# Matmuls of the slot counts behind the second pair's scores, and VectorE's offsets and slots one iteration later, in a fused patch embedding, attention and expert kernel

## The chip, the core and the metric

The kernel runs on one core of a Trainium2 chip: TensorE (matmuls into PSUM banks), VectorE, ScalarE and GpSimd, the queues that issue DMA (SyncE's above all), and 16 DMA engines. Each engine works through its own instructions in the order in which they are written; semaphores tie the engines together. The metric is the device time of the core in microseconds (us), lower is better.

## What is computed

32 images of 224x224 are cut into 16x16 patches, embedded into 192 numbers each, put along a Hilbert curve of 256 places and joined with 77 text tokens: 333 tokens an image. Then comes a block of convolutional attention and a block of experts, each behind a layer norm and added to its input. Cut to what matters:

```python
h = concat([patch_embed(x)[:, hilbert], txt], 1)            # (32, 333, 192)
q = layernorm(h)
key  = pointwise(depthwise9(q)) + pw_b                      # 12 heads of 16
w    = softmax(einsum(key * q, ak_w) + ak_b)                # 9 taps per head
v    = q @ pt_w.T + pt_b
h    = h + sum_k w[..., k] * shift(v, k)
f    = layernorm(h)
scores, idx = top_k(f @ Wg, 2); weights = softmax(scores)   # 8 experts
for k in range(2):                                          # capacity 1598 each
    pos = cumsum(onehot(idx[:, k])) - 1                     # place within the expert
    buf[e, pos] = token (dropped beyond capacity)
    ye  = (f[buf] @ W1a * silu(f[buf] @ W1b)) @ W2
    out = out.at[buf].add(w_buf * ye)
```

The running count over all tokens (`cumsum`) gives each token its slot in an expert's list. It goes on from group to group: the order of the groups is fixed by it.

## The kernel before

There are two stages. The first makes rows and slots (to about 830 us), the second runs tiles of 256 slots through the experts. The change lies in the first.

The first stage works in 16 **pairs** of images (p) and 8 **groups** of four images (g). Iteration `it` of its loop runs pairs p = 2it and p + 1 through embedding, transposes, convolutions, values and scores; beside it VectorE runs the window sums of group it - 1, and the routing of group h = it - 2 is under way. Every engine has this loop written out in an order of its own.

TensorE, per iteration: for each of three tiles t, `conv(p, t)` (nine taps of 333 columns into `bankK`) and `values(p, t)` (into `bankV`); `transposes(p + 1)`; `patch(p + 2)` (48 matmuls into `bankH`); the three chunks of `scores(p, c)` into `bankN`; then the same for p + 1, with the transposes and the logits of group h between the taps of two convolutions; `transposes(p + 2)`, `patch(p + 3)`; `counts_before(h)` (L1090, L1091), two small matmuls that sum the counts over partitions into columns 448 to 479 of `bankN`; and `scores(p + 1, c)` (L1049). Logits, scores and counts share `bankN`. So `scores` waits before its first chunk until VectorE has read the logits (`lg_read`) and the counts (`pre_read`), and each chunk waits until ScalarE has emptied the one ahead (`kern_evac`).

VectorE, per iteration: `attend(p, 0)` (L666 reads `bankK`, L671 reads `bankV`), `norm(p + 1)` (L644, L652, L658), `part(2)`, `attend(p, 1)`, `softmax_top(it - 1)` (L693, L695, L697), `attend(p, 2)`, `part(14)`, `softmax_end` (L703 to L707), `attend(p + 1, 0)`, `norm(p + 2)`, `part(6)`, `attend(p + 1, 1)`, `part(8)`, `attend(p + 1, 2)`, `top_two(h)` (L761 to L790: the two best experts, their difference `gap` at L784, the counts `cnt` at L789), `part(2)`, `offsets(h)` (L796, L797: reads the counts out of `bankN` and adds `pre_read`), `places(h)` (L805 to L847: slots and weights of each token, `idx_ready`), `part(7)`. `part(n)` takes n steps of the window sums: a product (L713), a sum (L731), or the statistics of a finished slice (L748, L755). 39 steps an iteration are all that a group has, plus one; they are in two slices.

ScalarE, per iteration: `normalise(p + 1)`, the exponential of the window softmax (L563), the copies out of the transposes' banks (`tiles_out`, L519), `scores_out(p)` (L528, L530), the normalising of a slice (L540), copies for the router (L559), `normalise(p + 2)`, `tiles_out(p + 2)`, the gate's exponential of `gap` (L567), `scores_out(p + 1)`, `high_parts` (L549), and the next slice.

GpSimd, per iteration: layer norms of a pair or a slice (four small steps, L405 to L411), `low_parts` (L428, L429) and the 22 scatters (L129) of group it - 3, which wait for `idx_ready`, in two portions of 7 and 15. SyncE stores each pair's rows once its scores are emptied and loads the windows of a group behind both stores.

## Time and profile before

| | us |
|---|---|
| runs (three) | 1452.49, 1452.85, 1455.80 |
| median | 1452.85 |
| the profiled execution | 1455.03 |
| its span in the profile | 1453.2 |
| first stage, until the expert stage's first matmul | 836.5 |
| distance of the counts (L1090) of two iterations | 79.8, 81.4, 81.0, 79.9, 76.0 |

The profiled execution is one of its own. Its durations are read in the rows below, and the 1.8 us between its time and its span lie outside the records. A row of the timeline has its start, its length, the engine, the line and operation, what is written and read, how often it comes in a row, and in brackets how long the engine had been idle and what ended that. Mean granted TensorE clock of the whole execution: 0.907 of full speed.

### The profile page before, as it was taken

What the parts mean: (1) busy time and instruction counts of PE and PEld (TensorE: products, weight loads), DVE (VectorE), ACT (ScalarE), POOL (GpSimd) and SP (SyncE); (2) the same over time, 40 slices, a digit from 0 to 9 for tenths busy, and PEclk for the clock granted to TensorE, in tenths of its full rate; (3) what the DMA queues carried; (4) which work ended last, traced back from release to release, by engine and by line L of the source; (5) the groups of instructions that cost most, each with busy time, mean ns of one, the idle gap of its engine ahead of it and who ended that gap; (6) DMA issues with size and microseconds to landing.
All of it is one profiled execution on the core that took longest, in us unless ns stands there. A gap on an engine that the chain in (4) does not pass through costs nothing. (4 is left out here: it accounts for less than half of the span.)

```text
span 1453.2 us, 30800 instructions
## 1 busy us (share of the span) xinstructions
PE 1206.9 (83%) x8700; PEld 1012.7 (70%) x8701; DVE 1017.8 (70%) x2367; ACT 463.6 (32%) x1197; POOL 694.9 (48%) x530
## 2 busy tenths in 40 slices
PE   6987988998989898960642099999999999999995
PEld 6766777775767677640422078988898898898895
DVE  4117958999999999999576266666666666666663
ACT  2111222323223232311112254444444444444442
POOL 1000221666656666755647625544545454555454
PEclk9999999898999899885675599999999999999998
DMA  9995554565646363548611175544444444444442
GB/s 314 401 320 135 141 151 113 161 177 166 169 119 196 101 187 84 162 98 220 190 46 49 48 131 67 65 58 59 64 63 55 65 57 63 57 63 58 62 60 28
DMA packets 215171, 175.31 MB, mean 121 GB/s; under 512 B 121864, under 2 KB 198694, under 8 KB 215104
## 3 DMA queue, kind: packets, MB, share of 16 engines
q1 hardware_dynamic: 170128, 115.36, 32.7%
q0 software_dynamic: 34720, 34.38, 14.3%
q10 hardware_dynamic: 10256, 24.73, 4.6%
q8 instruction: 36, 0.59, 0.2%
q14 instruction: 31, 0.25, 0.1%
HBM read 69.24 MB, written 88.47 MB: 109 GB/s over the span
## 5 line engine op out<-in xcount | busy, mean ns | idle before, releaser
L1239 POOL DMA_INDIRECT out<-yb,meta x182 | 301.5, 1657 | 314.0 <-DMA out<-yb,meta 207.2
L129 POOL DMA_INDIRECT expert_inputs<-slot_rows,slots x176 | 236.5, 1344 | 85.5 <-issue 60.1
L1023 PE MATMUL bankK<-normedT,conv_w 128*128 128x333 f32 x864 | 277.2, 469 | 0.0
L1312 DVE TENSOR_TENSOR hidden<-silu,bankU 128x256 f32<-128x256 f32 x364 | 153.0, 421 | 136.6 <-PE bankU L1352 90.3
L1268 ACT ACTIVATE silu<-bankG 128x256 f32<-128x256 f32 x364 | 139.1, 383 | 301.7 <-PE bankG L1352 301.6
L1023 PEld LDWEIGHTS bankK<-normedT,conv_w 128*128 128x128 f32 x864 | 168.8, 201 | 77.7 <-issue 12.1
L1365 PE MATMUL bankY<-expert_weights,hidden_high 128*128 x728 | 179.2, 246 | 0.9 <-issue 0.2
L1366 PE MATMUL bankY<-expert_weights,hidden_high 128*128 x728 | 179.3, 246 | 0.0
L1367 PE MATMUL bankY<-expert_weights,hidden_low 128*128 x728 | 179.1, 246 | 0.0
L713 DVE TENSOR_TENSOR prod<-window_values,kb 128x960 f32<-128x960 f32 (+1 forms) x135 | 167.8, 1252 | 3.6
L731 DVE TENSOR_TENSOR hidden_group<-hidden_group,prod 128x960 f32<-128x960 f32 (+1 forms) x135 | 169.0, 1252 | 0.5
L1306 DVE TENSOR_TENSOR hidden_low<-hidden,hidden_high 128x256 f16<-128x256 f32 x364 | 153.1, 421 | 12.6
L1264 ACT CAST hidden_high<-hidden 128x256 f16<-128x256 f32 x364 | 145.2, 399 | 49.2 <-DVE hidden L1312 49.1
L1348 PE MATMUL bankG<-xeT,expert_weights 128*128 128x256 f16 x364 | 99.9, 275 | 68.5 <-DMA xeT<-expert_inputs 58.0
L1001 PE MATMUL bankH<-wp_sb,patches 128*128 128x192 f32 x768 | 138.7, 345 | 10.3 <-DMA tokb_sb<-in_tokb 10.3
L405 POOL TENSOR_TENSOR tmp<-mean_var,pool_constants 128x6 f32<-128x6 f32 (+1 forms) x32 | 24.3, 760 | 255.6 <-DVE mean_var L658 233.5
L1001 PEld LDWEIGHTS bankH<-wp_sb,patches 128*128 128x128 f32 x768 | 135.5, 204 | 9.9 <-DMA tokb_sb<-in_tokb 9.9
L1288 DVE TENSOR_SCALAR yb<-bankY,slot_weight 128x192 f32<-128x192 f32 x182 | 67.5, 412 | 62.4 <-PE bankY L1367 62.4
L1348 PE MATMUL bankU<-xeT,expert_weights 128*128 128x256 f16 x364 | 100.0, 275 | 0.0
L1352 PE MATMUL bankG<-xeT,expert_weights 128*128 128x256 f16 x364 | 99.7, 274 | 0.0
L1350 PE MATMUL bankG<-xeT,expert_weights 128*128 128x256 f16 x364 | 99.7, 274 | 0.0
L1349 PE MATMUL bankG<-xeT,expert_weights 128*128 128x256 f16 x364 | 99.7, 274 | 0.0
(162 smaller groups left out, 2294.9 us busy)
## 6 DMA issues: line engine op xcount, KB each, us to landing
patches<-in_x SPq DMA_DIRECT2D x16, 1536.0 KB, 8.9
expert_inputs<-prod ACTq DMA_DIRECT2D x6, 3430.0 KB, 23.3
token_rows<-rowbuf SPq DMA_DIRECT2D x32, 492.0 KB
window_values<-token_rows SPq DMA_DIRECT2D x32, 264.0 KB, 5.5
hidden_group<-token_rows SPq DMA_DIRECT2D x32, 264.0 KB, 7.1
window_values<-token_rows SPq DMA_DIRECT2D x32, 192.0 KB, 5.7
kb<-token_rows SPq DMA_DIRECT2D x32, 148.5 KB, 4.7
token_rows<-rowbuf SPq DMA_DIRECT2D x32, 148.0 KB
```

What stands on the lines that cost most here:

```text
L129: nc.gpsimd.indirect_dma_start(out=xslots[:, :], out_offset=bass.IndirectOffsetOnAxis(ap=idx[g % 2][:, k, r:r + 1], axis=0), in_=xrow[g % ...
L713: return V.tensor_tensor(to[:, 0:(hi - lo) * D].rearrange("p (a d) -> p a d", d=IPG), vx[g % 2][:, (lo + k) * D:(hi + k) * D].rearrange("p ...
L731: added[k] = done(V.tensor_tensor(acc, acc, prod[k % 2][:, 0:(hi - lo) * D], ALU.add))
L1001: mm = T_.matmul(bankH[c][:, m * D:(m + 1) * D], xb[u][:, m, kc * TI + c * 128:kc * TI + c * 128 + 128], wp_sb[:, kc, :], start=(kc == 0), ...
L1023: mm = T_.matmul(bankK[(u + t) % 2][:, 0:L], conv_w[:, t // 2, k, :], qT[u][:, t, k:k + L], start=(k == 0), stop=(k == K - 1))
L1239: nc.gpsimd.indirect_dma_start(out=out[:, :], out_offset=bass.IndirectOffsetOnAxis(ap=meta[t % NMETA][:, c, 0:1], axis=0), in_=yb[v][:, c, ...
L1306: V.tensor_tensor(hl[v][:, j, :], hf[j % 2][:, :], hh[v][:, j, :], ALU.subtract)\
L1312: V.tensor_tensor(hf[j % 2][:, :], sg[j % 2][:, :], bankU[j][:, 0:TS], ALU.mult)\
L1348: T_.matmul(o, w(0, lo), high, start=True, stop=False)
L1365: T_.matmul(o, hh[v][:, j, cs], w(0, j), start=(j == 0), stop=False)
L1366: T_.matmul(o, hh[v][:, j, cs], w(1, j), start=False, stop=False)
L1367: mm = T_.matmul(o, hl[v][:, j, cs], w(0, j), start=False, stop=(j == NJ - 1))
```

## The change

On TensorE the counts of group h move behind the three chunks of `scores(p + 1)`. They then wait until ScalarE has emptied the last chunk (`2 * g + 6` pairs of `kern_evac` in place of `2 * g + 5`). `scores` no longer waits for the counts of its own iteration to be read, but for those of the iteration before, now in both pairs. On VectorE, `offsets` and `places` of a group are made in the following iteration, behind `norm(p + 1)`; `part(2)` and `part(7)` become `part(9)`. Those of group 5 come behind the loop, ahead of the rest of group 6's window sums.

```diff
--- before.py
+++ after.py
@@ -927,6 +927,9 @@
                     attend(p, 0)
                     if it:
                         norm(p + 1)
+                    if it > 2:
+                        offsets(h - 1)
+                        places(h - 1)
                     if it > 1:
                         part(2)
                     attend(p, 1)
@@ -949,13 +952,11 @@
                     attend(p + 1, 2)
                     if it > 1:
                         top_two(h)
-                    part(2)
-                    if it > 1:
-                        offsets(h)
-                        places(h)
-                    part(7 if it > 1 else 13)
+                    part(9 if it > 1 else 15)
 
                 g, h = NG - 1, NG - 2
+                offsets(h - 1)
+                places(h - 1)
                 part(2 * NSL * K)
                 softmax_top(g)
                 softmax_end(g)
@@ -1041,9 +1042,10 @@
                     u = p % 2
                     pe.wait_ge(ca_done, 3 * p + 3)
                     wait(pe, kern_evac, 3 * p + c)
-                    if c == 0 and p > 3 and p % 2:
-                        pe.wait_ge(lg_read, p // 2 - 1)
-                        pe.wait_ge(pre_read, p // 2 - 1)
+                    if c == 0 and p > 3:
+                        if p % 2:
+                            pe.wait_ge(lg_read, p // 2 - 1)
+                        wait(pe, pre_read, p // 2 - 2)
                     T, n = CT[c], HA * K
                     for t in range(3):
                         mm = T_.matmul(bankN[0:T, t * n:(t + 1) * n], ca[u][:, t, 128 * c:128 * c + T],
@@ -1086,7 +1088,7 @@
 
                 def counts_before(g):
                     pe.wait_ge(cnt_ready, g + 1)
-                    pe.wait_ge(kern_evac, 3 * min(2 * g + 5, NPAIR))
+                    pe.wait_ge(kern_evac, 3 * min(2 * g + 6, NPAIR))
                     T_.matmul(bankN[:, CN:CN + 16], low_sb[:, :], cnt[:, :], start=True, stop=True)
                     T_.matmul(bankN[:, CN + 16:CN + 32], ones[:, 0:128], cnt[:, :], start=True, stop=True)\
                       .then_inc(pre_ready, 1)
@@ -1120,10 +1122,10 @@
                         transposes(p + 2)
                     if p + 3 < NPAIR:
                         patch(p + 3)
+                    for c in range(3):
+                        scores(p + 1, c)
                     if it > 1:
                         counts_before(h)
-                    for c in range(3):
-                        scores(p + 1, c)
 
                 g, h = NG - 1, NG - 2
                 for _ in logits(h, NPAIR):
```

TensorE at the end of an iteration's second pair, from the counts to the next pair's first convolution (`bankN` holds scores, logits and counts). Before:

```order
L1090 MATMUL bankN<-cnt,lower_sb 128x16 [waits kern_evac,cnt_ready]
L1091 MATMUL bankN<-cnt,ones 128x16
L1049 MATMUL bankN<-akA_sb,conv_attn_64 128x72 [waits lg_read,pre_read,kern_evac,ca_done]
L1049 MATMUL bankN<-akA_sb,conv_attn_64 128x72
L1049 MATMUL bankN<-akB_sb,conv_attn_64 128x72
L1049 MATMUL bankN<-akA_sb,conv_attn_64 128x72 [waits kern_evac,ca_done]
L1049 MATMUL bankN<-akA_sb,conv_attn_64 128x72
L1049 MATMUL bankN<-akB_sb,conv_attn_64 128x72
L1049 MATMUL bankN<-akA_sb,conv_attn_64 77x72 [waits kern_evac,ca_done]
L1049 MATMUL bankN<-akA_sb,conv_attn_64 77x72
L1049 MATMUL bankN<-akB_sb,conv_attn_64 77x72
L1023 MATMUL bankK<-normedT_61,conv_w 128x333 [waits ca_done,qT_done]
```

And with the change:

```order
L1051 MATMUL bankN<-akA_sb,conv_attn_64 128x72 [waits lg_read,pre_read,kern_evac,ca_done]
L1051 MATMUL bankN<-akA_sb,conv_attn_64 128x72
L1051 MATMUL bankN<-akB_sb,conv_attn_64 128x72
L1051 MATMUL bankN<-akA_sb,conv_attn_64 128x72 [waits kern_evac,ca_done]
L1051 MATMUL bankN<-akA_sb,conv_attn_64 128x72
L1051 MATMUL bankN<-akB_sb,conv_attn_64 128x72
L1051 MATMUL bankN<-akA_sb,conv_attn_64 77x72 [waits kern_evac,ca_done]
L1051 MATMUL bankN<-akA_sb,conv_attn_64 77x72
L1051 MATMUL bankN<-akB_sb,conv_attn_64 77x72
L1092 MATMUL bankN<-cnt,lower_sb 128x16 [waits kern_evac,cnt_ready]
L1093 MATMUL bankN<-cnt,ones 128x16
L1024 MATMUL bankK<-normedT_61,conv_w 128x333 [waits ca_done,qT_done]
```

The two counts matmuls stand behind the nine of the scores now, and the first score matmul keeps its four waits, `pre_read` with a smaller number.

VectorE from the end of `top_two` to the second attend of the next iteration (`off` and `base` are the first steps of `offsets`, `token_numbers` the last of `places`, `stats<-rowbuf` belongs to `norm`). Before:

```order
L790 SCALAR_TENSOR_TENSOR running_count<-ones,onehot_valid 128x176
L731 TENSOR_TENSOR hidden_group<-hidden_group,prod 128x1152 [waits vector_step]
L713 TENSOR_TENSOR prod<-window_values,kb 128x1152 [waits vector_step]
L796 TENSOR_TENSOR off<-bankN,base 128x16 [waits pre_ready]
...
L847 TENSOR_SCALAR token_numbers<-token_numbers 128x11
...
L748 BN_STATS stats<-hidden_group 128x6 [waits vector_step]
...
L666 SCALAR_TENSOR_TENSOR conv_attn_63<-bankK,pwb_sb,normedT_61 128x333 [waits kern_ready,key_ready]
...
L644 TENSOR_TENSOR rowbuf_58<-bankH,tokb_sb 128x2x192 [waits h_ready,row_stored1]
...
L658 BN_AGGR mean_var<-stats 128x2 x5
...
L666 SCALAR_TENSOR_TENSOR conv_attn_63<-bankK,pwb_sb,normedT_61 128x333 [waits kern_ready,key_ready]
```

And with the change:

```order
L790 SCALAR_TENSOR_TENSOR running_count<-ones,onehot_valid 128x176
L731 TENSOR_TENSOR hidden_group<-hidden_group,prod 128x1152 [waits vector_step]
L713 TENSOR_TENSOR prod<-window_values,kb 128x1152 [waits vector_step]
...
L748 BN_STATS stats<-hidden_group 128x6 [waits vector_step]
...
L666 SCALAR_TENSOR_TENSOR conv_attn_63<-bankK,pwb_sb,normedT_61 128x333 [waits kern_ready,key_ready]
...
L644 TENSOR_TENSOR rowbuf_58<-bankH,tokb_sb 128x2x192 [waits h_ready,row_stored1]
...
L658 BN_AGGR mean_var<-stats 128x2 x5
L796 TENSOR_TENSOR off<-bankN,base 128x16 [waits pre_ready]
...
L847 TENSOR_SCALAR token_numbers<-token_numbers 128x11
...
L666 SCALAR_TENSOR_TENSOR conv_attn_63<-bankK,pwb_sb,normedT_61 128x333 [waits kern_ready,key_ready]
```

The 22 steps from `off` to `token_numbers` have gone from ahead of the slice's statistics to behind the norm, past the first attend; the second attend has the same steps ahead of it as before. ScalarE, GpSimd and SyncE keep their orders.

## Rows read from the trace of the kernel before

**Rows 1.** The page: busy time, share of the span and instructions of each engine.
```profile
PE 1206.9 (83%) x8700; PEld 1012.7 (70%) x8701; DVE 1017.8 (70%) x2367; ACT 463.6 (32%) x1197; POOL 694.9 (48%) x530
```

**Rows 2.** Windows: us, busy time of five engines, TensorE clock, DMA share, GB/s.
```profile
250.00:330.00 80.00, 72.39 (x356) 57.55 (x356) 76.22 (x144) 23.09 (x57) 49.65 (x41) 0.91 0.57 157
...
492.00:572.00 80.00, 72.57 (x353) 57.30 (x354) 76.29 (x143) 23.09 (x57) 51.39 (x43) 0.91 0.51 140
```

**Rows 3.** Waits of VectorE, 250 to 650 us: total us, times, longest.
```profile
DVE kb L693 <- DMA window_values<-token_rows: 1.9, 3, 0.9
DVE rowbuf L671 <- PE bankV L1037: 1.7, 4, 0.7
DVE stats L652 <- DMA rowbuf<-in_txt: 1.6, 1, 1.6
...
DVE conv_attn L666 <- PE bankK L1023: 1.2, 1, 1.2
```

**Rows 4.** Waits of TensorE, 250 to 650 us.
```profile
PE bankN L1049 <- DVEq L799: 13.8, 5, 2.8
```

**Rows 5.** Timeline of TensorE (start, us, work), two stretches of scores.
```profile
531.71 0.56 PE L1049 MATMUL bankN<-akA_sb,conv_attn 128*128 128x72 f32 x4
...
535.00 6.89 PE L1023 MATMUL bankK<-normedT,conv_w 128*128 128x333 f32 x18
...
563.02 8.01 PE L1001 MATMUL bankH<-wp_sb,patches 128*128 128x192 f32 x48
571.88 0.40 PE L1090 MATMUL bankN<-cnt,lower_sb 128*128 128x16 f32 x2 [0.85 <-DVE cnt L789]
...
575.26 0.64 PE L1049 MATMUL bankN<-akA_sb,conv_attn 128*128 128x72 f32 x4 [2.76 <-DVEq L799]
...
579.77 6.70 PE L1023 MATMUL bankK<-normedT,conv_w 128*128 128x333 f32 x18
```

**Rows 6.** Timeline of VectorE around offsets and places.
```profile
570.94 0.16 DVE L784 TENSOR_TENSOR gap<-m 128x11 f32<-128x11 f32 x1
...
574.82 0.16 DVE L796 TENSOR_TENSOR off<-bankN,base 128x16 f32<-128x16 f32 x1
...
578.94 1.35 DVE L731 TENSOR_TENSOR hidden_group<-hidden_group,prod 128x1152 f32<-128x1152 f32 x1
```

**Rows 7.** Timeline of ScalarE, the window softmax's exponential.
```profile
521.94 1.20 ACT L563 ACTIVATE kb<-kb 128x1188 f32<-128x1188 f32 x1 [0.15 <-DVE kb L697]
```

**Rows 8.** Timeline of TensorE, the last transpose of the first half.
```profile
361.11 0.82 PE L1013 MATMUL bankT<-identity,normed 128*128 128x128 f32 x3 [2.13 <-ACT normedT L519]
361.72 9.24 PE L1001 MATMUL bankH<-wp_sb,patches 128*128 128x192 f32 x48
...
523.52 0.51 PE L1013 MATMUL bankT<-identity,normed 128*128 128x128 f32 x3 [0.88 <-ACT normedT L519]
```

**Rows 9.** Windows: the clock behind that wait.
```profile
361.00:364.00 3.00, 2.89 (x10) 2.89 (x11) 2.93 (x4) 0.83 (x3) 2.69 (x2) 0.50 0.18 63
```

**Rows 10.** Timeline of VectorE at four places.
```profile
381.09 0.57 DVE L666 SCALAR_TENSOR_TENSOR conv_attn<-bankK,pwb_sb,normedT 128x333 f32<-128x333 f32 x1 [1.24 <-PE bankK L1023]
...
519.59 2.32 DVE L697 TENSOR_TENSOR kb<-kb,kmax 128x1188 f32<-128x1188 f32 x1
...
671.78 2.59 DVE L731 TENSOR_TENSOR hidden_group<-hidden_group,prod 128x960 f32<-128x960 f32 x1
...
684.02 0.44 DVE L755 BATCH_NORM_AGGREGATE mean_var<-stats 128x2 f32<-128x6 f32 x5
```

**Rows 11.** Timeline of GpSimd at four places.
```profile
519.02 1.64 POOL L429 TENSOR_TENSOR slot_rows<-group_normed,slot_rows 128x768 f16<-128x768 f32 x1
...
660.17 1.02 POOL L405 TENSOR_TENSOR tmp<-mean_var,pool_constants 128x6 f32<-128x6 f32 x1 [0.17 <-DVE mean_var L755]
...
670.80 2.55 POOL L429 TENSOR_TENSOR slot_rows<-group_normed,slot_rows 128x768 f16<-128x768 f32 x1
...
693.30 0.22 POOL L405 TENSOR_TENSOR tmp<-mean_var,pool_constants 128x5 f32<-128x5 f32 x1
```

## The prediction

> **What bounds the kernel now.** I first read the busy line of the page [rows 1]: TensorE 83%, VectorE 70% of the whole span. That average hides two stages. The change touches only the first 830 us, so the windows of single iterations of the first loop come next [rows 2]: from 250 us on, VectorE is busy 76 of every 80 us and TensorE 72. What VectorE does with the other 4 us is in its list of waits [rows 3]. From 250 to 650 us, five iterations, it waits 6.4 us for anybody: 1.9 for window loads, 1.7 for `bankV`, 1.6 for the text load, 1.2 for `bankK`. The rest, some 2 to 3 us an iteration, are the small gaps between dependent steps of its own. So **VectorE sets the length of iterations 3 to 7**, and TensorE's stalls are time that it has to spare. TensorE does wait, 13.8 us in five places, for exactly what the change takes away [rows 4]. But an engine that waits because another is full gains only what the full one gives back.
>
> **The stall that is removed.** In the iteration that ends at 579.77, TensorE finishes the patch matmuls at 571.03, gets the counts in at 571.88, idles 2.76 us until VectorE has read them (two window steps stand ahead of that read), and starts the scores at 575.26 and the next convolution at 579.77: 8.74 us [rows 5]. With the scores first, the first chunk can start at 571.1. The second needs ScalarE to empty `bankN`, and ScalarE has the gate's exponential ahead of that copy in its own order. That exponential waits for `gap`, which VectorE has at 571.10 [rows 6]. From there 0.2 us of exponential, 0.45 of copies, two more chunks as in the first pair's scores (531.71 to 535.00 for all three, 3.29 us [rows 5]), then a new wait: the counts need the last chunk emptied (some 0.6 us), and take 0.6 themselves. The convolution starts at 576.0 to 577.0, **2.8 to 3.8 us earlier**. Queued behind the counts' new wait are only that convolution and what follows it.
>
> **The steps that are moved on VectorE.** Offsets and places take from 574.82 to 578.94, 4.12 us [rows 6]. They are neither shorter nor fewer, and the two window steps that stood ahead of them stay. The second half of the group's first slice, its statistics, the first attend and the norm of the next iteration all come 4.12 us earlier; from the second attend on VectorE stands where it stood. Is the first attend's data there 4.12 us earlier? It began right when `bankV` was ready before; now the convolution starts at 576.0 to 577.0, takes 6.7 us at the mixed clock [rows 5] and 1.3 for the values, so 584.0 to 585.0, and VectorE wants `bankV` at about 584.8. It just fits: 0, bounds 0 to +1.5 for five iterations. The counts themselves were written 8 us or more before offsets now reads them: no wait. GpSimd's scatter needs the slots that places makes. It stands behind a layer norm and two subtractions there, and places ends about when that norm does: nothing.
>
> **Where the lead goes.** Behind the third convolution TensorE transposes the next pair. The last of the three transposes needs a bank that ScalarE empties, and ahead of that copy ScalarE has the window softmax's exponential, which waits for VectorE's subtraction, ending at 521.9. That time has not moved. So the exponential still starts at 521.94 [rows 7] and the last transpose, which waited 0.88 us at 523.52 [rows 8], still starts there: the wait grows to 4 to 5 us and **the lead is gone**. Window loads are the exception: they hang on the stores behind the second pair's scores, so they arrive 3 to 5 us earlier, and VectorE's waits for them go: **-1.9 us** [rows 3] (bounds 0 and -1.9). Its other waits hang on work behind that transpose and stay.
>
> **A price of the longer idle.** After 2.13 us without work at 361.11 [rows 8] the granted clock is 0.50, that is 1.2 instead of 2.4 GHz, until 364 [rows 9]. The patch matmuls took 9.24 us there and 8.01 in the other iteration [rows 5, 8]. VectorE then waited 1.24 us for `bankK` [rows 10] and 0.67 for `bankV`, where others have 0.36 in all: 1.55 us more. A wait of 4 to 5 us will do the same in iterations 3, 5 and 6 (4 has it already; 7 has no patch matmuls and 5 us of slack): 3 x 1.55 = **+4.65 us**. Bounds: 0 if the clock holds, and twice the row's price in those three and once more in 4, 7 x 1.55 = +10.9.
> The Trainium skill ("TensorE: Matmul & The Clock Gate", HAM oscillation) says the same: an idle gap between bursts re-throttles the array, and the next burst starts cold each time. By that rule this term is certain and the slower case below gains; by the shorter waits of the trace alone it could be left at 0.
>
> **GpSimd against VectorE.** VectorE's subtraction of 1188 elements took 2.32 us at 519.59 against 1.40 at other places, while GpSimd's L429 ran to 520.66 [rows 10, 11]: 0.92 lost, and 4.7 us over the five iterations, 0.94 each. At 671.78 a window step of 1.15 us took 2.59 beside L429 [rows 10, 11], and the one before it lost 0.6: 2.04 in all. These subtractions of GpSimd follow its layer norm, which starts with the norm of VectorE and so now 4.12 us earlier. They meet the steps of places, many of them with two inputs, instead of a reduction and one subtraction. Between 0.94 and 2.04 I take the middle, 1.49: 5 x 0.55 = **+2.75 us**, bounds -4.7 (they miss each other) and 5 x 1.10 = +5.5.
> The Trainium skill ("SBUF — State Buffer", Who interferes with whom) gives the reason: a VectorE instruction with two SBUF inputs and a GpSimd instruction that reads SBUF take turns on one port, and whoever comes second waits for the whole instruction. The rows agree, and by the rule a chain of small two-input steps can lose to both subtractions, which is the upper bound.
>
> **The end of the first stage.** Here the move does help. In the last iteration places of group 5 stood ahead of the statistics of group 6's first slice, and now stands behind them. GpSimd's norm of that slice starts at 660.17 and would start at 656.1. Behind it follow on GpSimd the low parts and seven scatters, and only then the norm of the second slice, at 693.30, although VectorE had its input at 684.46 [rows 10, 11]. On this norm hang ScalarE's exponential of the last group, VectorE's last windows, and the scatters that hold back the expert stage. Ten us of slack on VectorE's side, so all of it moves: **-4.1 us**. SyncE's weight loads also start some 5 us earlier (the last scores are emptied at 651.7 instead of 656.9), and the 8.6 us hole in the scatters goes with them; bounds -4.1 and -5.2.
>
> **The sum.** -1.9 + 4.65 + 2.75 - 4.1 = +1.4 us. The profiled execution took 1455.03 us (span 1453.2), 2.2 above the median of 1452.85; a difference carries over, so 1452.85 + 1.4 = **1454.2 us**. A measurement here can tell about 0.3%, 4.4 us, from no change.
>
> **Rivals.**
> 1. Neither clock nor port costs anything. Then -1.9 - 4.1 = -6.0 gives 1446.9, and with all of VectorE's waits gone and the end at its bound -6.4 - 5.2, 1441.3. For it: the clock held through the waits of 1.4 us. Against: it fell after 2.1, and 4 to 5 are longer. 0.16.
> 2. TensorE is the bound after all, and the 2.8 to 3.8 us count in each of four iterations: 4 x 3.3 + 4.1 = 17.3, so 1435.5. Against it stand 6.4 us of VectorE waits in 400. 0.04.
> 3. Slower. The transposes' idle time costs a long slow stretch each time: +10.9 + 2.75 - 1.9 - 4.1 = +7.65, 1460.5; with the port at its bound 1463.3. It decides once the losses of the loop pass 4.4 + 6.0 = 10.4 us, which is 2.1 us an iteration. For it: the clock has only two levels, and a longer idle time can put the whole patch group and the scores behind it at the lower one. 0.20.
> 4. The change does not do what it says: ScalarE's order holds the scores back as long as the counts did, nothing moves in the loop, and only the end gains: 1448.7. 0.05.
> The forecast has 0.55. Faster by over 0.3%: rivals 1 and 2, 0.20. Slower: rival 3, 0.20. Within: 0.60. The range that leaves out one in ten at either side runs from inside rival 1, 1445.5, to inside rival 3, 1461.5.
>
> **What would show it.** In the profile after: no wait of TensorE's scores for VectorE's queue; a wait of 4 to 5 us of the last transpose for `normedT`, with the granted clock at 0.5 behind it; patch matmuls of the first half at 9 us or more; VectorE's waits for `bankK` at four iterations instead of one, and none for window loads; its busy time an iteration up by 0.5; counts 80 to 83 us apart; the norm of the last but one group's second slice 4 us earlier beside VectorE's last window step. I am wrong if iterations become shorter than 79 us (TensorE's lead reached VectorE), or if that norm stays where it was.

## The result and the profile after

The kernel before takes 1452.49 us (median of 7 runs, 1450.62 to 1455.8) and the changed kernel **1460.14 us** (7 runs, 1454.15 to 1462.41): ratio 1.0043, 95% interval 1.0028 to 1.0057, so 6.2 us more by the ratio (the medians are 7.7 apart). The forecast was 1454.2, 1.4 us more. A second pair gave 1.0025 (1.0011 to 1.0039), and a third, on another chip than the second, 1.0127 (1.0106 to 1.0147). The change is slower each time, and in the third by far the most; both want an explanation.

Each group of four experiments below ran on one chip, beside the kernel before. The median of the kernel before was 1461.60 us in the first group, 1454.48 in the second and 1454.31 in the third. The profiled execution of the changed kernel took 1454.15 us, its fastest; that of before took 1455.03, one of its slower ones. So the two traces differ by 0.9 us only, and I compare stretches of them, not their ends. A further trace of each comes from one chip (`before_again`, 1454.21, and `again2`, 1459.37).

The busy line of the changed kernel's page answers to [rows 1]:

```profile
PE 1202.0 (83%) x8700; PEld 1009.5 (70%) x8701; DVE 1024.8 (71%) x2367; ACT 463.3 (32%) x1197; POOL 671.4 (46%) x530
```

GpSimd has 23 us less, VectorE 7 us more. VectorE's step `gap` (L784) marks the same work in each iteration, and the five iterations that the prediction spoke of lie between the `gap` of iteration 2 and that of iteration 7, the last. Windows from mark to mark (us, busy time of each engine, TensorE's granted clock, DMA share, GB/s), first before and `before_again`, then after and `again2`:

```profile
248.91:646.89 397.98, 348.73 (x1655) 272.91 (x1655) 377.41 (x697) 110.56 (x273) 252.80 (x206) 0.91 0.54 148
```

```profile
246.28:645.85 399.57, 349.90 (x1655) 273.25 (x1655) 378.62 (x698) 110.62 (x273) 252.37 (x206) 0.90 0.54 147
```

```profile
246.47:651.35 404.88, 346.17 (x1655) 271.72 (x1655) 383.71 (x698) 110.05 (x273) 228.20 (x206) 0.92 0.53 145
```

```profile
247.41:654.69 407.28, 347.40 (x1660) 272.98 (x1659) 383.68 (x698) 110.11 (x273) 227.70 (x206) 0.92 0.53 145
```

The loop is **6.9 us longer** in the first pair (`before`, `after`) and 7.7 in the second (`before_again`, `again2`), and VectorE's busy time alone has grown by 6.3 and 5.1 us. Where it grew is in the groups by line of the same stretches, before and then after:

```profile
L731 DVE TENSOR_TENSOR hidden_group<-hidden_group,prod 128x1152 f32<-128x1152 f32 x45 | 60.7, 1348 | 0.2
...
L697 DVE TENSOR_TENSOR kb<-kb,kmax 128x1188 f32<-128x1188 f32 x5 | 11.1, 2217 | 0.2
...
L825 DVE TENSOR_TENSOR pos<-onehot_valid,merged 128x176 f32<-128x176 f32 x5 | 1.7, 342 | 0.2
...
L831 DVE TENSOR_SCALAR keep<-posk 128x22 f32<-128x22 f32 x5 | 0.8, 167 | 0.0
```

```profile
L731 DVE TENSOR_TENSOR hidden_group<-hidden_group,prod 128x1152 f32<-128x1152 f32 x45 | 63.1, 1401 | 0.2
...
L697 DVE TENSOR_TENSOR kb<-kb,kmax 128x1188 f32<-128x1188 f32 x5 | 7.0, 1395 | 0.2
...
L831 DVE TENSOR_SCALAR keep<-posk 128x22 f32<-128x22 f32 x5 | 5.6, 1125 | 0.0
L825 DVE TENSOR_TENSOR pos<-onehot_valid,merged 128x176 f32<-128x176 f32 x5 | 5.5, 1093 | 0.2
```

The softmax's subtraction (L697) lost its delay, 4.1 us in all, and the softmax's first step (L693) another 0.6, which that step had in one iteration. Two steps of places took the delay over and more: L825 went from 0.34 to 1.09 us and L831 from 0.17 to 1.13, 8.6 us in all. And two window adds (L731) beside GpSimd's subtractions for the second slice take 3.2 us instead of 2.7, five times, 2.4 in all. Together that is the 6.3 us. GpSimd in one of these places, and VectorE beside it:

```profile
512.97 0.91 POOL L428 TENSOR_TENSOR slot_rows<-group_normed,slot_rows 128x384 f16<-128x384 f32 x1
513.84 1.74 POOL L429 TENSOR_TENSOR slot_rows<-group_normed,slot_rows 128x768 f16<-128x768 f32 x1
```

```profile
512.99 1.09 DVE L825 TENSOR_TENSOR pos<-onehot_valid,merged 128x176 f32<-128x176 f32 x1
...
514.49 1.13 DVE L831 TENSOR_SCALAR keep<-posk 128x22 f32<-128x22 f32 x1
```

From the first step of offsets to the last of places it is now 5.74 us instead of 4.05, in each of the five iterations. VectorE's waits, as in [rows 3]:

```profile
DVE stats L652 <- DMA rowbuf<-in_txt: 5.1, 4, 1.4
...
DVE rowbuf L671 <- PE bankV L1038: 1.4, 4, 0.4
```

The waits for window loads are gone, and so is the one for `bankK`; one of 0.5 us for a store of rows is new. But the **text load** now holds it up four times, 5.1 us instead of 1.6. TensorE, as in [rows 4]:

```profile
PE bankT L1014 <- ACT normedT L519: 18.7, 9, 3.5
...
PE bankV L1036 <- DVE rowbuf L671: 12.5, 5, 2.7
```

The 13.8 us behind `offsets` are gone; what the lead ran into stands here. The last transpose of each first half waits 3.55 us for ScalarE, `values(p, 2)` 2.4 to 2.7 us for VectorE's second attend. What follows that transpose, to be held against [rows 5, 8]:

```profile
525.47 0.51 PE L1014 MATMUL bankT<-identity,normed 128*128 128x128 f32 x3 [3.55 <-ACT normedT L519]
525.82 9.69 PE L1002 MATMUL bankH<-wp_sb,patches 128*128 128x192 f32 x48
...
538.59 5.25 PE L1024 MATMUL bankK<-normedT,conv_w 128*128 128x333 f32 x18
```

```profile
520.00:534.00 14.00, 12.10 (x76) 10.91 (x74) 13.83 (x13) 4.52 (x12) 12.11 (x7) 1.00 0.36 140
534.00:546.00 12.00, 11.49 (x46) 8.08 (x46) 11.10 (x25) 3.53 (x10) 3.73 (x5) 0.86 0.70 213
```

```profile
520.00:534.00 14.00, 10.45 (x55) 9.84 (x55) 13.79 (x14) 2.30 (x4) 7.68 (x5) 0.88 0.12 42
534.00:546.00 12.00, 10.84 (x56) 8.39 (x55) 11.18 (x20) 3.49 (x11) 1.78 (x4) 1.00 0.44 148
```

The first two windows are of the kernel before, the last two of the changed one. The patch matmuls take 9.69 us where [rows 5] has 8.01, with a granted clock of 0.88 over these 14 us instead of 1.00. But the convolution behind the scores, which took 6.89 us at 0.86, now has 1.00 and takes 5.25. **In this iteration, number 6, the clock falls once either way, only earlier.**

In the trace of before, iterations 3 and 6 have the fall behind the scores. Iteration 5 has it at the patch matmuls already, behind a wait of 0.88 us, and iteration 4 has two falls. The patch matmuls of iteration 4 and the convolution behind its scores, then the patch matmuls of iteration 5:

```profile
361.00:371.00 10.00, 9.89 (x54) 9.89 (x54) 9.83 (x10) 0.83 (x3) 8.78 (x5) 0.84 0.14 48
374.00:381.00 7.00, 7.00 (x24) 4.60 (x22) 5.49 (x13) 2.69 (x7) 1.78 (x4) 0.76 0.75 250
442.00:452.00 10.00, 9.94 (x53) 9.94 (x53) 9.83 (x10) 0.78 (x3) 8.78 (x5) 0.83 0.13 47
```

In the first trace of the changed kernel iterations 3 to 6 all have 0.83 at the patch matmuls and 1.00 behind the scores. The mean over the whole loop, in the windows from mark to mark above, is 0.92 in both traces of the changed kernel, 0.91 and 0.90 in those of before: in these two pairs the change costs no clock.

The end of the stage, to be held against [rows 10, 11]:

```profile
651.35 0.16 DVE L784 TENSOR_TENSOR gap<-m 128x11 f32<-128x11 f32 x1
```

```profile
692.33 0.86 POOL L405 TENSOR_TENSOR tmp<-mean_var,pool_constants 128x5 f32<-128x5 f32 x1
```

```profile
836.73 0.39 PE L1350 MATMUL bankG<-xeT,expert_weights 128*128 128x256 f16 x1 [57.98 <-DMA xeT<-expert_inputs]
```

From the last `gap` of the loop to GpSimd's norm of the last slice there are 41.0 us instead of 46.4. To the first matmul of the expert stage there are 185.4 instead of 189.6 (836.45 less 646.89 before), and 186.1 instead of 190.8 in the second pair.

### The profile page after: what moved, and what is told of

Same layout as the page of the kernel before. It is cut to its first block and busy times, and to the rows that moved or that the text cites. A ratio compares the mean times of both kernels' runs of the same rounds, so it can differ in the third digit from the quotient of the medians.

```text
span 1452.4 us, 30799 instructions
## 1 busy us (share of the span) xinstructions
PE 1202.0 (83%) x8700; PEld 1009.5 (70%) x8701; DVE 1024.8 (71%) x2367; ACT 463.3 (32%) x1197; POOL 671.4 (46%) x530
## 5 line engine op out<-in xcount | busy, mean ns | idle before, releaser
L129 POOL DMA_INDIRECT expert_inputs<-slot_rows,slots x176 | 220.1, 1251 | 91.8 <-issue 60.2
L731 DVE TENSOR_TENSOR hidden_group<-hidden_group,prod 128x960 f32<-128x960 f32 (+1 forms) x135 | 171.5, 1271 | 0.5
L405 POOL TENSOR_TENSOR tmp<-mean_var,pool_constants 128x6 f32<-128x6 f32 (+1 forms) x32 | 20.9, 652 | 307.6 <-DVE mean_var L658 234.3
L1002 PEld LDWEIGHTS bankH<-wp_sb,patches 128*128 128x128 f32 x768 | 136.5, 205 | 10.2 <-DMA tokb_sb<-in_tokb 10.2
```

The lines of the kernel that those rows point to most:

```text
L129: nc.gpsimd.indirect_dma_start(out=xslots[:, :], out_offset=bass.IndirectOffsetOnAxis(ap=idx[g % 2][:, k, r:r + 1], axis=0), in_=xrow[g % ...
L731: added[k] = done(V.tensor_tensor(acc, acc, prod[k % 2][:, 0:(hi - lo) * D], ALU.add))
L1002: mm = T_.matmul(bankH[c][:, m * D:(m + 1) * D], xb[u][:, m, kc * TI + c * 128:kc * TI + c * 128 + 128], wp_sb[:, kc, :], start=(kc == 0), ...
```

## Experiments

**again.** The changed kernel, unaltered, in the first group.

> The changed kernel once more, unaltered, for a second trace: its first trace was of a run of 1454.15 us, while its median was 1460.14. Theory A (clock): typical runs are slower because the granted clock falls behind the longer wait of the last transpose at 0.5 and stays there over the patch matmuls, so that VectorE waits for bankK in three iterations or more, 1 to 1.5 us each; then this trace, if its run took 1458 us or more, shows L671 or L666 waiting for bankK for 3 us or more between 250 and 650 us. Theory B (text load and port): no bankK wait again, VectorE's waits for the text load 5 us in all, places 5.7 us instead of 4.05 in every iteration, and the extra of a typical run lies outside the first loop. Ratio to the kernel before under both 1.003 to 1.006.

1481.42 us, ratio 1.0127 (1.0106 to 1.0147), three times the excess of the first result and outside what both theories expected. VectorE's waits in the loop:

```profile
DVE stats L652 <- DMA rowbuf<-in_txt: 7.5, 4, 2.6
DVE conv_attn L666 <- PE bankK L1024: 6.6, 4, 2.3
DVE rowbuf L671 <- PE bankV L1038: 4.1, 8, 0.7
```

The waits for `bankK` that theory A asked for are there, but their cause is not the one it named. ScalarE and TensorE at the end of an iteration (`gap` at 505.12), and GpSimd's last scatter of the row:

```profile
505.32 0.21 ACT L567 ACTIVATE ex<-gap 128x11 f32<-128x11 f32 x1 [9.14 <-DVE gap L784]
509.71 0.28 ACT L528 COPY rowbuf<-bankN 128x144 f32<-128x144 f32 x1 [4.18 <-remote]
```

```profile
503.38 0.56 PE L1051 MATMUL bankN<-akA_sb,conv_attn 128*128 128x72 f32 x4
...
510.26 1.10 PE L1051 MATMUL bankN<-akA_sb,conv_attn 128*128 128x72 f32 x4 [6.09 <-ACT rowbuf L530]
...
514.81 1.46 PE L1024 MATMUL bankK<-normedT,conv_w 128*128 128x333 f32 x2
```

```profile
507.10 1.44 POOL L129 DMA_INDIRECT expert_inputs<-slot_rows,slots  x1 [0.30 <-issue]
```

The first chunk of scores is computed by 504.2 and ScalarE is free from 505.5, yet its copy starts at 509.71: 4.18 us in which nothing that the profile shows is missing. The convolution starts 9.7 us after `gap` instead of 4.3 in the first trace (578.45 after 574.14), and VectorE stands at the first attend. I call this the stall. It happens in iterations 3 to 6. In iterations 2 and 7, where no scatters are in progress, the copy follows the exponential at once, and in the first trace it does so always. The copy starts 1.1 to 1.3 us after the end of the last scatter, in all four.

The loop of this trace takes 421.85 us, 17.0 more than in the first. About 11 of these are VectorE's waits, and 5.9 are busy time (389.62 us instead of 383.71): GpSimd's subtractions for the second slice come later too and meet window steps of 960 elements, which take 110.5 us in all instead of 103.3.

**tail_only.** The kernel before with the last iteration of the change.

```diff
-                    if it > 1:
+                    if 1 < it < NG - 1:
                         offsets(h)
                         places(h)
...
                 g, h = NG - 1, NG - 2
+                offsets(h - 1)
+                places(h - 1)
                 part(2 * NSL * K)
...
-                    if it > 1:
+                    if 1 < it < NG - 1:
                         counts_before(h)
                     for c in range(3):
                         scores(p + 1, c)
+                    if it == NG - 1:
+                        counts_before(h)
```

> The kernel before with the change in its last iteration only: the counts of group 5 behind the last scores, and offsets and places of group 5 behind the loop; all earlier iterations are the kernel before. Theory A (the term of the end is real and separate): the distance from the last gap of the loop to GpSimd's norm of group 6's second slice falls from 46.4 us to 41 or 42, all but 1 us of it reaches the first expert matmul, and the time is 1447.5 to 1448.5 us, ratio 0.9965 to 0.9975. Theory B (something else is late next at the end: ScalarE's scores or the window sums of the last group): ratio 0.999 to 1.001. Theory C (the shorter end in the first trace was not the move but what the loop left behind, for instance its earlier stores): the distance stays at 45 to 46.

1455.39 us, ratio **0.9954** (0.9937 to 0.9970). The distance from `gap` (649.38) to the norm (691.97) is 42.6 us. Theory A holds for the distance and the sign; the gain was 6.2 us where it had said 4 to 5. The trace does not show where those arrive: from `gap` to the first expert matmul it has 192.6 us, more than `before` and `before_again` (189.6 and 190.8), but `again` has 192.9 on this chip, of whose kernel before there is no trace. VectorE waits 0.56 to 0.74 us for the counts in iterations 3 to 6 of this trace, as it does in neither of the two traces of before. There too it goes on 1.1 to 1.3 us after the last scatter.

**slots_first.** GpSimd's scatters ahead of its low parts.

```diff
-                    if it > 1:
-                        low_parts(it - 2, 0)
                     if it > 2:
                         scatter(it - 3, 0)
+                    if it > 1:
+                        low_parts(it - 2, 0)
```

> The changed kernel with one edit: in the loop GpSimd issues the first scatters of a group ahead of the low parts of the next group's first slice, and so begins these two subtractions only when VectorE has made the slots. Theory A (VectorE and GpSimd share a port, and places loses to these subtractions): the two steps that took 1.09 and 1.13 us take 0.34 and 0.17 again and places 4.1 us instead of 5.7 in all five iterations, 1.6 us each; if the subtractions then meet nothing as dear, 8 us less than the changed kernel; if the moved subtractions take from VectorE's maximum and subtractions of the softmax what they took before, 0.9 each, 3.5 us less (ratio 1.002 instead of 1.0043). Theory B (the longer steps come from something else, for instance their own place behind the norm): places stays at 5.7 and the time at ratio 1.004.

1473.62 us, 7.8 less than `again` on the same chip. Groups of `again` and then of this one:

```profile
L731 DVE TENSOR_TENSOR hidden_group<-hidden_group,prod 128x960 f32<-128x960 f32 x45 | 56.6, 1257 | 0.2
L713 DVE TENSOR_TENSOR prod<-window_values,kb 128x960 f32<-128x960 f32 x45 | 53.9, 1207 | 1.2
...
L831 DVE TENSOR_SCALAR keep<-posk 128x22 f32<-128x22 f32 x5 | 5.6, 1124 | 0.0
L825 DVE TENSOR_TENSOR pos<-onehot_valid,merged 128x176 f32<-128x176 f32 x5 | 5.5, 1092 | 0.2
```

```profile
L713 DVE TENSOR_TENSOR prod<-window_values,kb 128x960 f32<-128x960 f32 x45 | 60.5, 1354 | 1.2
L731 DVE TENSOR_TENSOR hidden_group<-hidden_group,prod 128x960 f32<-128x960 f32 x45 | 60.1, 1336 | 0.2
...
L825 DVE TENSOR_TENSOR pos<-onehot_valid,merged 128x176 f32<-128x176 f32 x5 | 1.7, 342 | 0.2
...
L831 DVE TENSOR_SCALAR keep<-posk 128x22 f32<-128x22 f32 x5 | 0.8, 163 | 0.0
```

Places is back at 4.03 us, 8.6 less in all. **GpSimd's subtractions are what places loses to.** Moved, they meet the window steps of the second slice and cost 10.1 us there, beyond the 7.2 that these steps lose in `again` already. VectorE's busy time is no smaller (390.93 us against 389.62), and still the kernel is faster, because places stands ahead of the softmax's subtraction. ScalarE waits 5.58 us for that instead of 7.29, the last transpose, the scores and the stores come earlier, and the waits for the text load fall from 7.5 to 2.1 us.

**patch_first.** TensorE's patch matmuls ahead of the transposes.

```diff
-                    transposes(p + 1)
                     if p + 2 < NPAIR:
                         patch(p + 2)
+                    transposes(p + 1)
```

> The changed kernel with one edit: TensorE does the patch matmuls of pair p+2 ahead of the transposes of pair p+1 instead of behind them, so the wait of the last transpose for ScalarE is filled with work. Theory A (that idle time costs through the clock and through the later scores, stores and text load): the 3.55 us wait goes below 0.5, the patch matmuls take 8 us or less instead of 9.7, the first pair's scores are ready 3 us earlier, VectorE's waits for the text load fall from 5.1 us to about 1.5 between 250 and 650 us, and the time is 3.5 us less than the changed kernel, or 7 where typical runs have bankK waits besides. Theory B (the transposes are now late for ScalarE's copies, which hold the second pair's convolution): VectorE waits for bankK or bankV 1 us or more in every iteration, 0 to 5 us more than the changed kernel.

1465.26 us, 16.2 less than `again` (ratio 1.0031, 1.0018 to 1.0045). The last transpose waits 0.24 us instead of 3.55, the scores of the first half start 41.6 us after `gap` instead of 46.7 (534.05 less 492.42, 551.78 less 505.12), and VectorE does not wait for the text load at all (7.5 before). What it still waits for is `bankK`, 8.2 us, and `bankV`, 2.9. I put that down to the stall at the end of the iteration, which shows on ScalarE in three iterations here. In the fourth TensorE itself starts its scores late, at 580.71, 1.10 us after the end of the last scatter, idle for 0.78 us before with nothing missing that the profile shows. So theory A holds for the chain from the transposes' wait to the text load, and the gain is twice the 7 us it allowed; what the other half is, no run separates.

**before_again, again2, three_parts, tail_three** (second group). The first two are unaltered. In the other two, four scatters move, in `three_parts` in the changed kernel and in `tail_three` in the kernel of `tail_only`. The same portions are issued behind the loop (not shown):

```diff
-            SC_AT = (0, 7, TOPK * R)
+            SC_AT = (0, 7, 11, TOPK * R)
...
                     if it > 1:
                         slice_norm(it - 2, 1)
+                    if it > 2:
+                        scatter(it - 3, 1)
                     if not last(2 * it + 1):
                         pair_norm(2 * it + 2)
                     if it > 2:
-                        scatter(it - 3, 1)
+                        scatter(it - 3, 2)
```

> The kernel before, unaltered, for a trace beside those of its neighbours. Theory A (a signal of TensorE given while GpSimd issues its row of scatters arrives only about 1.2 us after the last one, and the kernel before is hardly touched since its scores come later anyway): offsets is reached 3.7 us after the gate's exponential, or 4.3 to 4.5 where the signal of the counts is late, and ScalarE's first copy of the second pair's scores comes 5 to 6.5 us after that exponential as in its first trace; time 1451 to 1462 us. Theory B (one chip is simply slower in everything): VectorE's waits between 250 and 650 us grow by several us here too.

> The changed kernel, unaltered, a third trace. In the second one ScalarE stood still for 4.1 to 4.3 us in iterations 3 to 6 between the gate's exponential and the first copy of scores that had been computed 1 to 2 us before the exponential, and went on 1.1 to 1.3 us after the last of GpSimd's scatters each time; in the first trace it did not. Theory A (that stall is what the change exposes, and it makes the difference between the runs): traces with the four stalls take 15 us or more longer than the kernel before, and show VectorE waiting for bankK for 1.3 us or more in each of those iterations; those without it 0 to 3 us more than the kernel before. Theory B (the difference lies in the clock behind the transposes' wait): the time is large with or without the stalls.

1454.21 and 1459.22 us (ratio 1.0025). Neither shows the stall: from the start of the gate's exponential to offsets there are 3.68 us in `before_again`, and in `again2` 0.12 us to the start of the copy in iterations 3 to 6. Yet `again2` is 4.7 us above before by the medians, 3.6 by the ratio, where theory A had 0 to 3. The stall goes with the larger excess of the first group but is not all of it: without it 3 to 6 us are left.

> The changed kernel with one edit: four of GpSimd's fifteen later scatters of a group are issued behind the norm of the slice, where GpSimd has 7.8 us without work, so that the last of the row ends 5.2 us earlier, about 2 us before the gate's exponential instead of 1.4 to 3.4 us behind it. Theory A (the row of scatters holds TensorE's signal back): the copy follows the exponential at once (0.12 us) in every iteration, the scores, stores and text loads come 4 us earlier, and where the unaltered changed kernel shows the stalls the time is 9 to 13 us less than its; where it shows none, 0 to 2 us less. Theory B (ScalarE stalls there for a reason of its own, or because of what it executes): the stall of 4.2 us stays, and the time is that of the changed kernel within 2 us.

1460.24 us, ratio 1.0045 (1.0029 to 1.0061), against 1.0025 (1.0011 to 1.0039) for `again2`: no gain. On this chip there was no stall to take away, so nothing is said on theory A. It was not run on the chip that shows the stall, and **whether the scatters cause the stall stays open**.

> The kernel before with the change in its last iteration only, as in tail_only, and with four of the fifteen later scatters issued behind the slice's norm. Theory A: VectorE no longer waits for the counts (0.56 to 0.74 us in four iterations of tail_only), TensorE waits less for the read of the counts, the row of scatters ends earlier at the end of the stage too; 2 to 5 us less than tail_only, ratio to the kernel before 0.992 to 0.995. Theory B (the four scatters push the pair's norm late, since GpSimd had only 6.6 us free there, and with it normalise and the transposes): the time is that of tail_only or up to 3 us more.

1450.08 us, ratio **0.9972** (0.9962 to 0.9982), 4.1 us less than before by the ratio, and not the 0.992 to 0.995 expected; VectorE waits for no counts. `tail_only` ran on another chip, so whether the moved scatters add anything to the shorter end is not shown. From the last `gap` (645.06) to the first expert matmul (831.23) there are 186.2 us, 4.6 less than in `before_again` on the same chip: here the end's gain is seen to arrive.

**short_after, short_before** (third group): GpSimd's subtractions for the first slice of groups 0 to 5 shrunk to one column; the low parts of these rows stay zero.

```diff
-                    V.memset(xrow[n][:, :, META:XW], 0)
+                    V.memset(xrow[n][:, :, :], 0)
...
                     pool.wait_ge(xh_ready, NSL * g + s + 1)
+                    if s == 0 and g < NG - 2:
+                        nc.gpsimd.tensor_tensor(x16[:, ss, LOB:LOB + 1], xn[:, ss, 128:129], x16[:, ss, 128:129],
+                                                ALU.subtract).then_inc(xl_ready, 1)
+                        return
```

> The changed kernel, in which GpSimd's subtractions for the first slice of groups 0 to 5 write one column instead of 192 each row (the low parts of these rows stay zero, so what the experts receive is not the reference's). It takes away what places meets on GpSimd and nothing else. Theory A (the port): places takes 4.05 us instead of 5.74 in all five iterations, 8.5 us in all, and softmax_top comes as much earlier, with it the exponential, the last transpose, the scores and the text load: 8.5 to 11 us less than the changed kernel, ratio to the kernel before 0.996 to 0.998. Theory B (places is longer for another reason, or the time saved goes into waits): places stays at 5.74, or the ratio is 1.001 or more.

> The kernel before with the same shortened subtractions on GpSimd. Theory A: its VectorE meets them only in the softmax's last subtraction, 2.17 to 2.60 us instead of 1.40, so it gains 0.9 to 1.2 us an iteration, 4.5 to 6 us, ratio 0.996 to 0.997; the change is then worth 3 to 5 us on the port, the difference between the two savings, and the two shortened kernels come within 2 us of one another (the end saves 5, the text load costs 3.5). Theory B (the port is no part of the difference): both shortened kernels save the same, and their distance stays 4 to 6 us.

1448.95 us, ratio 0.9973 (0.9957 to 0.9990), and 1452.59 us, 0.9990 (0.9975 to 1.0005). The loop of short_before, then of short_after:

```profile
247.62:645.31 397.69, 344.23 (x1656) 269.64 (x1655) 373.17 (x697) 109.95 (x273) 230.85 (x201) 0.91 0.54 148
```

```profile
246.87:647.69 400.82, 349.47 (x1662) 274.80 (x1660) 375.48 (x697) 110.23 (x273) 214.31 (x201) 0.92 0.53 147
```

In `short_after` places is back at 4.05 to 4.08 us. With these subtractions gone from both, the change comes out **faster** than the kernel without it, by 3.6 us at the medians and 2.5 by the ratios, whose intervals overlap; with them it was 3.6 to 6.2 slower in the two pairs without the stall. Its loop is still 3.1 us longer (400.82 less 397.69). What makes it faster is the end: 185.9 us from the last `gap` to the first expert matmul, 190.8 in `short_before`.

On the busy time the subtractions cost 5.5 us in the kernel before (378.62 less 373.17; 4.2 by the trace `before`) and 8.2 in the changed one (383.68 less 375.48). What is left between the two short kernels, 2.3, is L731's. But the time they give back is 1.5 us in before, less than the 4.5 to 6 of theory A, and 7.6 or 10.2 after (0.9973 against 1.0025 and 1.0043). These are ratios of other groups, since the changed kernel itself did not run in this one, and with intervals of 2 us at either side the two sizes are rough. In before VectorE's gain went into waits: 5.1 us for the text load and 3.0 for `bankV`, where `before_again` has 2.5 and 2.1. So the text load is not a price of the change alone; it stands right behind VectorE in both kernels.

**pe_only** (third group). TensorE's half of the change; VectorE as before.

```diff
-                    if c == 0 and p > 3 and p % 2:
-                        pe.wait_ge(lg_read, p // 2 - 1)
-                        pe.wait_ge(pre_read, p // 2 - 1)
+                    if c == 0 and p > 3:
+                        if p % 2:
+                            pe.wait_ge(lg_read, p // 2 - 1)
+                        wait(pe, pre_read, p // 2 - 2)
...
-                    pe.wait_ge(kern_evac, 3 * min(2 * g + 5, NPAIR))
+                    pe.wait_ge(kern_evac, 3 * min(2 * g + 6, NPAIR))
...
+                    for c in range(3):
+                        scores(p + 1, c)
                     if it > 1:
                         counts_before(h)
-                    for c in range(3):
-                        scores(p + 1, c)
```

> TensorE's half of the change alone: the counts behind the scores, but VectorE makes offsets and places where the kernel before does. VectorE then waits for counts that come 4.5 us after the gate's difference instead of 1.4, at a place that it reaches after 3.9: 0.6 us or a little more in each iteration, or 4 to 5 where ScalarE's first copy of the scores is held back by GpSimd's scatters. Nothing of the port and nothing of the end's gain. Theory A (VectorE's half causes the loss in the loop and the gain at the end): the waits for window loads vanish (1 to 2 us), 3 us for the counts come, ratio 1.000 to 1.002. Theory B (TensorE's half costs by itself, because the earlier convolution leads to the longer wait of the last transpose and so to later scores and text loads): 1.003 or more.

1469.31 us, ratio **1.0112** (1.0086 to 1.0138). Waits of VectorE, and two steps of places:

```profile
DVE off L796 <- PE bankN L1092: 3.1, 5, 1.0
```

```profile
L812 DVE TENSOR_TENSOR pos<-running_count,off 128x176 f32<-128x176 f32 x5 | 5.0, 994 | 0.2
...
L808 DVE TENSOR_SCALAR w<-ex 128x11 f32<-128x11 f32 x5 | 4.0, 800 | 0.0
```

The counts come 0.4 to 1.0 us late, as both theories had it (3.1 us). The rest was in neither. The earlier scores make ScalarE's high parts and so GpSimd's subtractions for the second slice come earlier, and in this order these meet places. L812 takes 0.99 us instead of 0.34 and L808, eleven elements, 0.80 instead of 0.11: 6.7 us. These two make up the 9.8 us by which the loop (409.36) is longer than in `before_again`; the end has 1.5 more (192.3 instead of 190.8 us to the first expert matmul). Theory B's bound is met, but not by its cause. TensorE's half alone costs 15 to 16 us. The whole change cost 3.6 and 6.2 in the pairs without the stall, and this trace has no stall either, so VectorE's half seems to repair more than it costs. The changed kernel was not run in this group and cost 18.5 us where it met the stall, so that is not shown.

**mended** (third group). The changed kernel with the edits of patch_first, slots_first and three_parts.

> The changed kernel with three edits together: the patch matmuls ahead of the transposes, the slots' scatters ahead of the low parts, and four of the later scatters behind the slice's norm. Theory A (the move gains nothing in the loop even where all its side costs are removed, because VectorE is the bound there): VectorE waits less than 1 us an iteration, the iterations are 78 to 80 us as in the kernel before, and only the end's 5 us are left: ratio 0.996 to 0.998, no better than the version that changes the last iteration alone. Theory B (the side costs hid a gain of TensorE's): iterations below 78 us, ratio below 0.995. Theory C (the patch matmuls ahead of the transposes make VectorE wait for bankK, 1.2 to 2.7 us an iteration as in patch_first): ratio 1.000 or more.

1452.65 us, ratio 0.9991 (0.9978 to 1.0003).

```profile
244.01:645.53 401.52, 347.95 (x1655) 270.43 (x1655) 384.71 (x697) 109.95 (x273) 239.05 (x206) 0.92 0.52 147
```

```profile
DVE conv_attn L670 <- PE bankK L1028: 1.5, 1, 1.5
DVE rowbuf L675 <- PE bankV L1042: 0.9, 2, 0.7
```

VectorE waits 2.4 us for others in five iterations, and they are still 80.3 us each, in the kernel before 79.9: its busy time is 384.7, six more than before. Theory A holds for the cause: with the side costs gone from the waits, the loop is no shorter than before. The iterations are a little above its 80 us, and the interval of the ratio takes in 1, where it had said 0.996 to 0.998. GpSimd's subtractions cost 10.3 us at the window steps of the second slice, and the end's gain is there (185.5 us).

## Why the prediction was right and wrong

The time lies in the range and on the side of the forecast, but beyond what I called no change. That the loop's three terms add up to 5.5 us, near the measured 6.9 and 7.7, is luck: the largest, the clock, was worth nothing, and the port and the text load, which I had at 2.75 and 0, filled its place. Rival 3, the slower one, has the size but not the cause: it made the clock pay for it. By the terms:

- **Window loads, -1.9: right** [rows 3] (-1.0 in the second pair, which had no more). But "its other waits hang on work behind that transpose and stay" failed. The text load of pair p+2 hangs on the store behind the first pair's scores. Counted from `gap`, these start 43.2 us on instead of 40.7 in iteration 6 (535.34 less 492.14, 531.71 less 491.00; 0.8 to 2.7 us later in iterations 3 to 6): 1.7 from the patch matmuls at the lower clock and 0.8 from an exponential that comes later because places is longer. The store is 2.4 us later by the same count, the text load 2.0. VectorE's waits for it grow by 3.5 us (1.6 to 5.1) and 3.6 (2.5 to 6.1). I had looked at what TensorE's clock does to `bankK` and not at the queue behind the scores. patch_first shows the chain by breaking it.
- **The clock, +4.65: wrong, 0.** The wait, at 3.55 us instead of 4 to 5, the fall and the patch matmuls of 9.7 us came as forecast. The waits for `bankK` did not, in either undisturbed pair: VectorE's for `bankK` and `bankV` together are 3.0 and 1.4 in the first, 3.5 and 2.6 in the second. The step that failed is that I added the price of a second fall. I had it from iteration 4 [rows 8 to 10], the one iteration with two falls (0.84 and 0.76 in the windows above). Iteration 5 had the fall at the patch matmuls too, which I had missed; there VectorE waited 0.36 us for `bankV` and nothing for `bankK`. Nor does the length of the wait decide it, as I had argued, since the wait there was 0.88 us. With the change the fall at the patch matmuls takes the place of the one behind the scores, and the convolution gives back 1.6 us of the 1.7 that the patch matmuls lost. The Trainium skill ("TensorE: Matmul & The Clock Gate", HAM oscillation) was right on the cold burst behind the gap (9.69 us behind a wait of 3.55); whether it costs anything was a matter of what came next.
- **The port, +2.75: right in cause, too small.** The subtractions of the first slice moved from L697 to places as I had said, at +3.8 us in the first pair and +3.0 in the second (8.6 less 4.7 or 5.5 at L693 and L697). Two things were missing. Those of the second slice come earlier too and meet two window adds, +2.4, which makes 6.3 us in the first pair, above my bound of 5.5. And I counted the port at its busy time, though places stands ahead of `softmax_top`: a microsecond there delays ScalarE, TensorE and the text load as well. short_after and short_before give 6 to 9 us for the first slice alone, roughly (7.6 or 10.2 saved after, by the two ratios, less 1.5 before).
- **The end, -4.1: right.** -4.2 in the first pair, -4.7 in the second, and alone it is worth 4.1 to 6.2 us (tail_three, tail_only).
- **The first attend, 0 (bounds 0 to +1.5): right where ScalarE is not held up**, 2.1 to 3.0 us in each of four iterations where it is (again). The trace of before does not show that stall: its scores come 5 us after the exponential anyway.
- **GpSimd's scatter wait for slots, "nothing": wrong**, 1.8 us each, off the path.

In the loop, VectorE's busy time has 6.3 us more, its waits for the text load 3.5 more and for a store 0.5 more, those for window loads 1.9 less and for `bankK` and `bankV` 1.6 less: 6.8 of the measured 6.9. In the second pair the same five give 5.1 + 3.6 + 1.0 - 1.0 - 0.9 = 7.8 of 7.7.

With the end, the sum of what the traces show is 6.9 - 4.2 = +2.7 us in the first pair and 7.7 - 4.7 = +3.0 in the second, beside 6.2 (4.1 to 8.3) and 3.6 (1.6 to 5.7) by the ratios. The second sum fits. For the first pair 3.5 us are in no trace, since the profiled run was the fastest of its kernel; whether its other runs met the stall is not known, and these 3.5 us stay open.

## What to carry to other kernels

Moving a step on a full engine moves its neighbours too: list what a third engine runs beside the step at its new place, and what runs beside the steps that have moved with it, before counting the stall that goes. A loss ahead of the step that other engines wait for can cost more than its length: moving it behind that step saved 7.8 us here (slots_first), with no less busy time. When you price a side effect from one row of the trace before, look whether the other iterations have it too, and what it cost there. And if a change has an end effect and a loop effect, try the end alone: here one iteration's worth of the edit was the whole gain, 0.3 to 0.5%.

## What the runs showed of the hardware

VectorE instructions with one SBUF input were long beside GpSimd's two-input subtractions too. L831, a `tensor_scalar` on 22 elements, took 1.13 us instead of 0.17 and ended at 515.62, where GpSimd's L429 ended at 515.58; L808, on 11 elements, took 0.80 instead of 0.11. The Trainium skill ("SBUF — State Buffer", Who interferes with whom) names two SBUF inputs or a 2-port mode as the condition for VectorE, and `tensor_scalar` among the operations that can enter such a mode. These rows do not contradict it. Whether the one-input steps were in that mode and waited themselves, or stood behind a neighbour that did, the rows do not tell.

On one chip of those used, ScalarE's copy of finished scores was held back until 1.12 to 1.25 us after the end of GpSimd's row of scatters, in 11 of 12 iterations of three kernels (again, slots_first, patch_first); in the twelfth TensorE's scores themselves came late, 1.10 us after it. In the two other traces of the changed kernel (after, again2) it is in none. There the change cost 0.25 to 0.43%, here 1.3%, and no experiment has settled its cause.
